# A gated cross-attention block with eight experts on one core: shared pieces moved between TensorE's steps, group 1's queries made earlier, pad numbers packed in pairs

## The reference

```
x = x + tanh(g0) * attention(layernorm(x), ctx, mask; Wq, Wkv)      # 16 heads of 16
h = layernorm(x)                                                    # 2048 tokens
logits = h @ w_router; the top 2 of 8 experts, softmax of the two logits
moe    = sum of score * (silu(h @ fc1_left) * (h @ fc1_right)) @ fc2   over the two chosen experts
shared = (silu(h @ gate_w) * (h @ up_w)) @ down_w                   # inner width 512
x = x + tanh(g1) * (moe + shared)
```

## Time and profile before

| | |
|---|---|
| three runs | 346.18, 351.27, 352.37 us (median 351.27) |
| the profiled execution | 347.93 us, of which 346.0 us is the span from the first to the last instruction |
| TensorE busy / VectorE / ScalarE / POOL | 315.0 / 245.8 / 169.7 / 130.2 us |
| mean granted TensorE clock | 0.970 |
| attention, groups 0 to 7 | to about 170 us |
| first expert product | 207.47 us |
| last expert product, last output | about 311 us, 346 us |

### The profile page before, as it was taken

How to read it: one execution, slowest core, us unless ns; L and a number is a source line. 1 busy time by engine, 2 the same in 40 slices (tenths; PEclk the granted TensorE clock), 3 DMA queues, 4 the chain that set the end, 5 groups by cost and what they waited for, 6 DMA issues and landing times.

```text
span 346.0 us, 8077 instructions
## 1 busy us (share of the span) xinstructions
PE 315.0 (91%) x2505; PEld 256.5 (74%) x2505; DVE 245.8 (71%) x728; ACT 169.7 (49%) x322; POOL 130.2 (38%) x151
## 2 busy tenths in 40 slices
PE   8958998999898978878789969999999999999986
PEld 8746777878777856555447547989889888888875
DVE  5565176979997979739858996676766667643695
ACT  2533467666767555435666704544544445433231
POOL 4731033313255536250577008754343343331000
PEclk9985599999999999999999999999999999999999
DMA  8885267948374937410122411333333333202951
GB/s 218 265 226 170 69 204 158 266 127 247 117 201 149 228 125 192 150 63 3 47 94 92 143 56 50 96 98 101 100 104 92 93 108 93 75 28 75 420 175 61
DMA packets 33062, 46.52 MB, mean 134 GB/s; under 512 B 5472, under 2 KB 27108, under 8 KB 32515
## 3 DMA queue, kind: packets, MB, share of 16 engines
q1 hardware_dynamic: 24994, 26.15, 26.9%
q0 software_dynamic: 4320, 10.92, 9.6%
q10 hardware_dynamic: 3712, 8.98, 8.1%
HBM read 21.55 MB, written 12.62 MB: 99 GB/s over the span
## 4 chain that ended last, share of the span: by engine, by line
PE 46%; DVE 26%; issue 12%; POOL 5%; DMA 5%; ACT 2%; SPq 2%; another core or an unknown queue 1%; POOLq 0%; DVEq 0%
PE ps L1693 25%; DVE mx L937 4%; PE ps L1380 3%; PE ps L1399 3%; PE ps L1346 3%; POOL dispatched L515 3%; DVE x_all L1306 3%; DVE fc_lo L1149 3%; PE ps L1742 2%; PE ps L1665 2%; PE ps L1432 2%; PE ps L1359 2%; DMA stacks<-expert_rows 1%; DVE fc_lo L1155 1%; DVE st L898 1%
## 5 line engine op out<-in xcount | busy, mean ns | idle before, releaser
L571 POOL DMA_INDIRECT expert_rows<-v_s,slot_u x39 | 38.3, 981 | 58.7 <-ACT v_s L841 48.1
L937 DVE TENSOR_REDUCE mx<-ps 128x8 f32<-128x1024 f32 x32 | 39.1, 1223 | 19.2 <-PE ps L1399 18.5
L655 ACT ACTIVATE probs<-ps 128x1024 f32<-128x1024 f32 x32 | 32.6, 1019 | 18.9 <-PE ps L1432 18.9
L1256 DVE TENSOR_TENSOR act<-ps,sil 128x256 f32<-128x256 f32 x39 | 16.6, 425 | 30.1 <-ACT sil L834 22.6
L1693 PE MATMUL ps<-fc_hi,xs_hi 128*128 x78 | 34.2, 439 | 1.4 <-DVE xs_lo L1237 1.4
L834 ACT ACTIVATE sil<-ps 128x256 f32<-128x256 f32 x39 | 15.0, 385 | 41.0 <-PE ps L1693 39.9
L523 POOL TENSOR_TENSOR work<-work 128x512 bf16<-128x512 f32 x16 | 18.5, 1155 | 43.9 <-ACT work L624 43.9
L1693 PE MATMUL ps<-fc_hi,xs_lo 128*128 x78 | 30.8, 394 | 0.0
L1693 PE MATMUL ps<-fc_lo,xs_hi 128*128 x78 | 30.7, 394 | 0.0
L841 ACT ACTIVATE v_s<-ps,wt 128x256 f32<-128x256 f32 x39 | 18.5, 475 | 19.5 <-PE ps L1693 10.8
L1399 PE MATMUL ps<-stacks 96*128 96x128 bf16 x256 | 21.4, 231 | 6.4 <-DVE mx L937 5.3
(11 more groups left out here) (217 smaller groups left out, 833.8 us busy)
## 6 DMA issues: line engine op xcount, KB each, us to landing
stacks<-work SPq DMA_DIRECT2D x75, 128.0 KB, 4.6
xs_in<-dispatched SPq DMA_DIRECT2D x39, 129.0 KB
fc_s<-in_fc ACTq DMA_DIRECT2D x8, 512.0 KB, 3.6
stacks<-work POOLq DMA_DIRECT2D x18, 128.0 KB, 4.4
fc_s<-in_fc ACTq DMA_DIRECT2D x8, 256.0 KB, 4.2
stacks<-expert_rows SPq DMA_DIRECT2D x2, 1024.0 KB, 6.0
probs<-expert_rows SPq DMA_DIRECT2D x2, 1024.0 KB, 10.1
ctx_s<-in_ctx_t SPq DMA_DIRECT2D x8, 192.0 KB, 3.4
```

The lines of the kernel that those rows point to most:

```text
L571: nc.gpsimd.indirect_dma_start(ys, bass.IndirectOffsetOnAxis(dst_u[:, r:r + 1], 0), y_out[:, r, :], None, bounds_check=2 * T - 1, oob_is_e ...
L655: nc.scalar.activation(probs[:, 2 * j + h], ps_t, ACT.Exp, scale=HD ** -0.5).then_inc(probs_ok[j][h], 1)
L937: nc.vector.reduce_max(mx[:, j, 8 * h:8 * h + 8], ps_s, AX_X).then_inc(max_ok[j][h], 1)
L1256: nc.vector.tensor_tensor(act[:, par], ps[:, 2 + par, FI:2 * FI], sil[:, par], ALU.mult).then_inc(act_ok, 1)
```

## The change

1. **Start.** `queries(1)` goes ahead of `values_proj(1)` (into PSUM bank 2, as `queries(0)`), and its first piece, rest and second piece are made in step 2, ahead of `values_in(1)`; SyncE copies the first two pieces (`stack_q(1, 0)`, `stack_q(1, 1)`) before `max_rows(0, 0)`; `normed_t(2)` goes ahead of `scores(0, 1, 1)`. Three warm-ups of 10, 8 and 10 matmuls are put between the first groups' matmuls. VectorE does `maxima(0, 0, 0)` before `first_norm` of the last twelve blocks.
2. **Weight loads.** Expert e's `fc1` and `fc2` are loaded in step e + 3 instead of e + 2 (the last two in step 9), gate, up and down one step later too. Experts 6 and 7 of `fc1` count on a semaphore of their own.
3. **Routing.** `places` is cut in two: it now only reads the positions, and `slots` (four to six small operations) follows `norm2` and the second maxima. `weights` goes behind `pieces(s - 2, 1)`.
4. **Shared pieces.** Step 8 keeps pieces 0 and 1 only, one behind `scores(7, 0, 0)`, which moves ahead of `scores_t(6, 0, 1)`, and one behind `values(6, 0, 1)`; step 9 has 2 to 5; 6 to 15 lie behind the loop. All of `shared_1` now comes after `positions(7)`. `tanh_0(1)` and the gates of j = 1 and 2 move back, and j = 3 uses Silu itself, with one product on VectorE.
5. **Early highs.** `high_of_fc1` runs in the order 0, 1, 4, 5, 2, 3, 6, 7, three of them before `max_t(7, 1)`; `low_of_fc1(0)` moves before `places(7)`.
6. **Chunk 0's sums.** ScalarE copies them, times tanh(g1), from PSUM into `kept` (in `hid_0`) in one operation, and TensorE waits for that alone; VectorE adds them to x in four operations after `sum_and_add(1)`.
7. **Numbers.** The eight pad numbers are packed in four, two in a word (count + 4096 * count), and unpacked in SyncE's registers; the first five tiles' row numbers are read one by one, each before its own load, instead of five at once.

The core of the diff (the semaphores' names, `shared_0`'s calls and the steps' repeated conditions are cut):

```diff
         def expert_steps(eng, body, load=None, head=True):
...
-                pad_i[0:1, :], engines=[mybir.EngineType.SP], min_val=0, max_val=NULL_ROW - P)[1]
+                pad_i[0:1, 0:E // 2], engines=[mybir.EngineType.SP], min_val=0, max_val=T + COUNTS * T)[1]
             for e in range(E):
-                sp.dma_start(xs[bass.ds(pads[e], P), :], zrow[:, :]).then_inc(pad_out, 16)
+                filled = pads[e // 2] >> 12 if e % 2 else pads[e // 2] & (COUNTS - 1)
+                sp.dma_start(xs[bass.ds(filled + e * R, P), :], zrow[:, :]).then_inc(pad_out, 16)
...
+            for n in range(HEAD):
+                row = first_rows(0, n, 1)[0]
+                if n == 0:
+                    sp.wait_ge(scat[0], ALL_0)
+                    sp.wait_ge(scat[1], ALL_1)
+                    sp.wait_ge(pad_out, 16 * E)
+                load_tile(Tile(0, n), row)
...
+            def silu_0(j):
+                sa.wait_ge(g0_done, j + 1)
+                sa.wait_ge(hid0_ok, j)
+                nc.scalar.activation(sig_a[:, :], ps[:, BANKS_0[0], :], ACT.Silu).then_inc(sig_ok, 1)
...
+                if s == 2:
+                    second(1, kr_ok, k_rest, k_pc, k_ok[1])
+                    first(1, q_done, qst, q_pc, q_ok[0], ps_q0)
...
-                if live(s - 2):
-                    load_experts(s - 2)
+                if live(s - 3):
+                    load_experts(s - 3)
+                if s == G + 1:
+                    load_experts(E - 1)
...
             heads_out(g - 1, 1)
-            tanh_0(1)
+            high_of_fc1(0)
+            high_of_fc1(1)
+            high_of_fc1(4)
             max_t(g, 1)
             exp(g, 0, 0)
             second_row(g - 2, 1)
             exp(g, 0, 1)
             second_score(g - 2)
+            tanh_0(1)
...
             sa.wait_ge(down_done, CH)
+            nc.scalar.activation(kept, ps[:, BANKS_0[0]:BANKS_0[1] + 1, :].rearrange("p b c -> p (b c)"), ACT.Copy,
+                                 scale=tg[:, 1:2]).then_inc(sums_ok, 1)
...
             expert_rows(Tile(0, 0), 1)
             sum_and_add(1, CH, sums)
+            ve.wait_ge(sums_ok, 1)
+            for t in range(CH):
+                nc.vector.tensor_tensor(x_all[:, t, :], x_all[:, t, :], kept[:, D * t:D * t + D], ALU.add
+                                        ).then_inc(base_ok, 1)
             expert_act(Tile(0, 0), 0)
...
             values_proj(0)
+            warm(10)
             normed_t(1)
+            warm(8)
+            queries(1)
+            scores(0, 0, 0)
             values_proj(1)
-            scores(0, 0, 0)
             scores(0, 0, 1)
+            warm(10, 4)
...
                 if s == G:
-                    shared_0(2)
-                    shared_0(3)
+                    scores(s - 1, 0, 0)
+                    shared_0(0)
...
-            pe.wait_ge(base_ok, CH)
+            pe.wait_ge(sums_ok, 1)
```

## The result

The change made the kernel a little slower, not faster: 349.25 us (348.43 to 351.56, four executions) against 348.73 us (343.77 to 352.37, four) of the kernel before on the same chip, ratio 1.0127 [1.0084, 1.017]. On a second chip the same pair gave 1.0163 [1.009, 1.0236]. The profiled execution took 349.94 us, where 336.8 us were worked out. Ratios in this document leave out executions more than 1.5% above the fastest of their kernel, mostly those with the lowest clocks (in the first pair two of the four of before, hence 1.3% where the medians are 0.1% apart); medians leave out none.

The account below looks back on a forecast made before the run. TensorE, busy 315 of 346 us, was taken as the bound, with gains in its idle time and clock. 6.5 + 2 + 3.1 - 0.5 = 11.1 us off 347.9 gave 336.8, plus 1.2 about 338 us; range 331.5 to 346.

Parts of the forecast that it names:

- The sum is made against the profiled execution: Whole kernel: gains were subtracted from the one profiled execution, 347.93 us with 346.0 us of span.
- the start term: First groups: the new order takes half-clock queries off TensorE's path and keeps the clock up; 6.5 us gained, ends 3 and 8.
- The 1.2 us laid on for the median: Whole time: part of the 3.3 us by which the median exceeded the profiled execution, added to reach 338 us.
- the clock stays up, at three to one: Start: busier TensorE stretches keep the granted clock full, with `queries(2)` at 39 to 41 instead of 46.66 us.
- rival A: Start: the clock falls all the same, so the start is worth 3 us, not 6.5; 341.5 us, chance 0.15.
- Routing, 2 us: Steps 6 and 8: `slots` and `weights` leave the way of `norm2` and the last maxima; 2 us gained, ends 0 and 4.
- Shared pieces in step 8: Step 8 loses four pieces (3.9 us), which return behind the loop; TensorE idles some 3.3 us, step ends 0.5 to 1 earlier.
- rival B: Step 8: the clock falls at the 3.3 us hole, lasting 21 us as at the start; costs 8 us, 346 us, chance 0.13.
- Step 9 and the tail: Step 9 to first expert product: all idle time but 2.5 us filled; 3.1 us gained with step 8's 0.7, ends 0 and 6.
- rival D: Step 9: pauses stay or come elsewhere, so the tail gains only 0 to 1 us; 340.5 us, chance 0.15.
- Chunk 0's sums: First expert tiles: ScalarE's copy costs nothing, VectorE's four additions take 1.7 us; 0.5 us lost, ends 0 and 1.5.
- Weight loads and numbers: Later weight loads: zero. Pad and row numbers before the first tiles: zero, ends -0.5 (a gain) and 1 us.

Follow-up runs that it names:

- experiment 5: The kernel before, unchanged, traced again on a second chip: 336.99 us, ratio 1.0031.
- experiment 6: The changed kernel, unchanged, traced again on a second chip: 341.78 us, ratio 1.0163 against the kernel before.
- experiment 9: The kernel before with 34 further warm-up matmuls in TensorE's idle time ahead of its first scores: 339.82 us against 335.87, ratio 1.0102.
- experiment 11: The kernel before with the start part of the change alone, on another chip than its first run: 341.69 us against 335.87, ratio 1.0169.
- experiment 2: The changed kernel with VectorE's four additions later and shared pieces 0 and 1 ahead of `max_t(6, 1)` in step 8: 348.21 us, ratio 1.0011 against before.
- experiment 3: The kernel of experiment 2 with `gated_0(2)` moved ahead of `slots(6)` and `weights(6)`: 342.64 us against 344.14 of before, ratio 0.9916.
- experiment 12: The kernel of experiment 3 with the start put back as before: 338.77 us against 335.87 of the kernel before, ratio 1.0035.
- experiment 8: The kernel of experiment 3 with 14 more warm-up matmuls behind `scores(0, 1, 0)`, on another chip: 336.73 us, ratio 1.0017 against before.
- experiment 15: The kernel before, unchanged, for a trace at a higher mean clock: 336.58 us, clock 0.990.
- experiment 1: The changed kernel with VectorE's four additions moved to the ends of its steps of tiles 0 and 1: 345.51 us against 344.14 of before, ratio 1.0007.
- experiment 7: The changed kernel with POOL's three low halves waiting until VectorE's four additions are done: 343.77 us, ratio 1.0243 against before.
- experiment 10: The changed kernel with its start part put back as before: 347.45 us against 335.87 of the kernel before, ratio 1.0319.
- experiment 14: The kernel before with numbers, routing and chunk 0's kept sums, additions behind tiles 0 and 1: 337.56 us against 336.21, ratio 1.0063.

## Why the prediction was wrong

*"The sum is made against the profiled execution".* This is the step that failed first, and where most went: the sum took the low stretch of one execution for a standing cost of the kernel. That execution had a low stretch at the start as long as the longest of the four traces of the kernel before, and a chip with pauses. The 6.5 us of the start term were mostly the difference between it and two of the three others (`queries(2)` at 46.66 against 40.70 and 41.25 us; experiment 5 has 46.66 too), and the only other executions to hand, with their three times and no clocks, could not say so. The 1.2 us laid on for the median had no cause behind them, and the runs name none. One bound was also added up wrongly: with all terms at their lower ends (3 and 0 and 0 gained, 1.5 and 1 lost) the sum gives 347.4 us, not 346.

*Start, "the clock stays up, at three to one".* In the trace of after it fell at 28 us (rival A), and in experiment 6 it did not fall there, but at 91, 129 and 204 us. `queries(2)` came at 42.86 and at 37.98 us, on either side of the 39 to 41 given. What failed is the thought that a fall, once prevented, stays away: experiment 9 removed it with nothing changed but 34 warm-ups, and was slower. What the runs show in its place: with the new start the clock falls at 28 to 31 us in seven of nine traces, and `queries(2)` is then no earlier than it mostly is with the old one. Of the start alone (5.8 us) the fit puts 3.2 us on 9 us more of low clock and leaves 2.8 us, which may be the place of the low stretches (52.6 to 59.5 us in experiment 11) or the order; which was not found.

*Routing, 2 us.* Up to 1.4 us on the way and none at `down_0`; with the numbers the kernel is 0.7% slower in all (0.5% by the medians), by which of the two isn't shown.

*Shared pieces in step 8.* The hole was right in kind: 1.53 us for the DMA of group 7's queries where 3.3 us stood, and 1.72 us in experiment 6. The 2 to 3 us to land, counted from the end of an issue of 0.61 us, agree with the 3.4 us from its start that the trace of before has there (median of nine copies, 125 to 141 us). Of rival B the fall came, in both traces of after (134 to 141 and 129 to 136 us), for 7 us and not 21. I gave it 0.13. Its cause isn't shown: the clock fell 0.2 and 0.6 us into the hole, with the hole filled it fell all the same (136.4, 132.4 and 134.4 us in experiments 2, 3 and 12, not in 8), and it did so at 128.2 us in experiment 15, where nothing was changed. The 0.7 us given to step 8 did not come: without its four pieces it is 0.2 to 1.9 us longer.

*Step 9 and the tail, "if all idle time but 2.5 us is filled".* This is the second step that failed. On the first chip 5.9 + 2.9 us of idle time were counted and most of it was the chip's pauses. After still has 55.36 - 50.25 = 5.1 us idle from `scores_t(7, 0, 0)` to the first product against 6.8 before, so 1.7 us were filled and not 6.3; on a chip without pauses 0.3 us. What rival D says of pauses held. That TensorE bounds the stretch was right: VectorE ends its low parts 2.57 us ahead of the next `xs_lo`, and the wait of 1.39 us is gone.

*Chunk 0's sums, "0.5 us lost, ends 0 and 1.5".* Mis-sized: 3.5 us. The addition was priced by sixteen that took 0.415 to 0.425 us each, while POOL was idle or started DMAs; here one of the four began beside POOL's `down_lo`, set free earlier, and took 2.53 us. 1.65 us are TensorE's wait, the rest the fall that followed it. Experiment 1 shows what the additions cost where they stood, experiment 7 that POOL made the one long: apart from POOL's low halves none took more than 0.42 us.

*Weight loads and numbers.* Zero, as said, as far as the tiles go. The first fill goes out at 184.47 us and the first tile is requested at 192.68 us, 5 us earlier than in the earlier trace rows; the five requests take 12.61 us in place of 10.08, so the five loads cost 2.5 us where 3 were given, and nobody waited for a tile.

Why start and rest together cost less than the rest without it (1.6% against 3.2%) stays open: the two were on different chips and their clocks fell in different places. Of the 5.7 us between the medians of experiments 10 and 6 the fit puts 3.7 on 11 us more of low clock. That the start alone is slower is sure; by which wait is not.

## What to carry to other kernels

Before counting a low-clock stretch of a trace as something to gain, run the unchanged kernel several times and read each execution's mean clock: if most have a higher one, the gain is already in the median. Compare two kernels stage by stage, in several traces each, with the place of every low stretch beside it; an equal mean clock alone isn't enough. Idle time that one chip shows and another doesn't is no room for moved work; and when work moves between stages, the sum must have it at the place where it lands. Before an operation of VectorE is put where GpSimd has just been set free, ask what else the same signal starts: in all four traces here in which a kept addition began beside GpSimd's subtraction it took 1.42 to 2.53 us instead of 0.42.

## What was not expected of the hardware

The low-clock stretches move. The same program showed 20.5, 20.5, 3.4 and 10.2 us at its start, and a further one of 3.4 or 6.8 us in two of the four traces; of the kernels without one at the start experiments 6 and 9 got others of 3.4 to 6.8 us later, in experiment 9 in unchanged code, and experiment 8 got none. The cost is mostly 0.3 to 0.4 us for one of low clock on the mean, and up to 3.5 us for 7 in an attention step (experiment 11: `queries(2)` to `queries(3)` 20.2 us against 16.7).

ScalarE and VectorE have pauses of 2 to 5 us with no releaser in the traces of two measurements, worth 8 us of 340 (the kernels before and start alone have them at the same places), and, but for the 1.8 us at ScalarE's start, none over 1.2 us in those of three other chips. What they are I can't say.

One addition of 128 x 256 took 2.53 us beside POOL's subtraction (2.53, 2.51 and 1.42 us in experiments 6, 10 and 14) and 0.41 us without it, and each of the four ended 0.28 or 0.29 us after POOL.
